# Filler matmuls at the start, weight work moved within the first batches, and next x's maximum and x2's low part moved within the batch loop

## What is computed

```python
x = layernorm(x + L0(x, adj))    # y = (adj @ x + x) @ W0 + b0; y / |y|
x = layernorm(x + L1(x, adj))    # S = 8 tanh((xq)(xk)^T / sqrt(128) / 8); P = exp(S) * adj
                                 # (P / rowsum P) @ x @ v
x = layernorm(x + L2(x, adj))    # (s_i + s_j + adj * w_r + g_b) @ x @ W2 + b2
x = layernorm(x + L3(x, adj))    # relu(x@W3[0] + L@x@W3[1] + (2 L@L - 1)@x@W3[2] + b3)
```

## Time and profile before

| | |
|---|---|
| median of 3 runs | 712.55 us (712.53, 712.55, 714.25) |
| the profiled execution | 713.7 us |
| its span, first to last instruction | 711.4 us |
| TensorE busy | 636.5 us, 89% |
| VectorE busy | 589.1 us, 83% |
| ScalarE busy | 414.6 us, 58% |
| GpSimd busy | 74.0 us |
| mean granted TensorE clock | 0.97 of full |

### The profile page before, as it was taken

How to read it: one execution, slowest core, us unless ns; L and a number is a source line. 1 busy time by engine, 2 the same in 40 slices (tenths; PEclk the granted TensorE clock), 3 DMA queues, 4 the chain that set the end, 5 groups by cost and what they waited for, 6 DMA issues and landing times. The chain is left out here.

```text
span 711.4 us, 17445 instructions
## 1 busy us (share of the span) xinstructions
PE 636.5 (89%) x7398; PEld 477.7 (67%) x7398; DVE 589.1 (83%) x1521; ACT 414.6 (58%) x711; POOL 74.0 (10%) x49
## 2 busy tenths in 40 slices
PE   4598577899899998999899998999899999879894
PEld 2355444559666895669666895769666995548794
DVE  5868998778898898998898888998898888879535
ACT  6369559425584657836593658646693649423512
POOL 0111110002000210012001100012001100021002
PEclk9899888999999999999999999999999999989998
DMA  9520000001000020002000020002000010000102
GB/s 333 188 89 1 1 1 1 1 1 33 1 1 2 2 61 1 2 1 61 2 2 2 2 61 1 1 2 61 1 2 2 2 32 1 2 0 3 31 3 60
DMA packets 12446, 18.75 MB, mean 26 GB/s; under 512 B 592, under 2 KB 9040, under 8 KB 12368
## 3 DMA queue, kind: packets, MB, share of 16 engines
q1 hardware_dynamic: 12368, 17.63, 7.5%
HBM read 13.44 MB, written 4.19 MB: 25 GB/s over the span
## 5 line engine op out<-in xcount | busy, mean ns | idle before, releaser
L238 POOL TENSOR_TENSOR small<-small,minus_half 128x8 f32<-128x8 f32 x39 | 69.6, 1788 | 616.0 <-DVE small L564 317.8
L836 DVE TENSOR_TENSOR att<-att,adjT 128x1024 f32<-128x1024 f32 x64 | 78.1, 1221 | 16.2 <-ACT att L385 15.7
L383 ACT ACTIVATE att<-r,coef 128x1024 f32<-128x1024 f32 x64 | 70.4, 1101 | 18.7 <-PE r L1213 18.1
L841 DVE SCALAR_TENSOR_TENSOR p_lo<-p_hi,att 128x1024 f16<-128x1024 f16 x64 | 77.9, 1220 | 0.0
L279 ACT ACTIVATE p_hi<-att 128x1024 f16<-128x1024 f32 x64 | 66.9, 1045 | 18.2 <-DVE att L836 18.2
L1211 PE MATMUL r<-xq,a_hi 128*128 128x128 f16 x448 | 76.0, 219 | 0.0
L1212 PE MATMUL r<-xq,a_hi 128*128 128x128 f16 x448 | 76.0, 219 | 0.0
L1213 PE MATMUL r<-xq,a_lo 128*128 128x128 f16 x448 | 76.0, 219 | 0.0
L1211 PE MATMUL r<-rs,a_hi 128*128 128x128 f16 x448 | 75.8, 219 | 0.0
L1212 PE MATMUL r<-rs,a_hi 128*128 128x128 f16 x448 | 75.8, 219 | 0.0
L1213 PE MATMUL r<-rs,a_lo 128*128 128x128 f16 x448 | 75.8, 219 | 0.0
(11 more groups left out here) (380 smaller groups left out, 2092.7 us busy)
## 6 DMA issues: line engine op xcount, KB each, us to landing
adjT<-in_adj_t SPq DMA_DIRECT2D x8, 512.0 KB, 8.3
x<-in_x SPq DMA_DIRECT2D x7, 512.0 KB, 4.7
out<-outb SPq DMA_DIRECT2D x7, 512.0 KB, 3.4
pq<-in_adj SPq DMA_DIRECT2D x2, 512.0 KB, 8.3
u<-in_adj SPq DMA_DIRECT2D x2, 512.0 KB, 9.3
tmp<-in_adj SPq DMA_DIRECT2D x2, 512.0 KB, 10.0
x2s<-in_adj SPq DMA_DIRECT2D x2, 512.0 KB, 10.5
outb<-in_x SPq DMA_DIRECT2D x1, 512.0 KB, 11.3
```

What stands on the lines that cost most here:

```text
L238: return nc.gpsimd.tensor_tensor(dst, src, minus_half[:], ALU.pow)
L383: nc.scalar.activation(att[:, s], dst[:], ACT.Tanh, scale=c_tanh).then_inc(S["th"], 1)
L836: tt(att[:, s], att[:, s], adjT[:, t, :], ALU.mult).then_inc(S["pm"], 1)
L841: stt(p_lo[:, s], p_hi[:, s], -LO_UP, att[:, s], ALU.mult, ALU.add).then_inc(S["pl"], 1)
```

## The change

It moves instructions within the lists of the engines, and adds a few:

- TensorE: filler matmuls (`keep_busy`) of 512 columns, whose result nothing reads: 9 before the first x maximum's sum, 2 after it, 11 before the first product of x, 15 after layer 0's first projection. The first weights' sum stands ahead of chunk 3 in place of chunk 4, the second (w2, w3) ahead of the second scores of batch 0, layer 0's projection of batch 1 ahead of them too, and the sum for x of batch 2 in batch 1's attention.
- The factor in front of the exponential is no longer its bias: ScalarE multiplies adjT by it in place (`scale_adj`, eight copies, each after that chunk's a_lo is made).
- ScalarE: `v_scaled(0)` and the last row sum stand behind the first exponential; the row sums are taken in groups of 3, 3, 1, 1; `bias_rows` moves from batch 1's attention to the start of `back(1)`.
- VectorE, start: y of batch 1 and the scales of w2 and w3 stand ahead of and just behind the first mask, the weights of layer 3 in the wait for the first root and their maxima behind the splits of m and v, the first norm's shift ahead of batch 1's y0 low part; the maximum of x of batch 2, and the splits of w2 and w3, move from between the batches into batch 1's attention.
- VectorE, every `back`: the maximum of x of batch i + 2 ahead of the second `end_sum` (it stood at the start of the next front), and `x2_lo` ahead of `ln_shift(0, i + 1)` (it stood at the end).

```diff
         coef = sb("coef", [P, 8])
-        c_w0, c_tanh, c_v, c_l2, c_u, c_o, c_exp = (coef[:, j:j + 1] for j in range(7))
+        c_w0, c_tanh, c_v, c_l2, c_u, c_o = (coef[:, j:j + 1] for j in range(6))
         deg, dis, dis2, root_deg, eps_deg, r_scale, q_scale = (sb(n_, [P, C]) for n_ in ("deg", "dis", "dis2", "root_deg", "eps_deg", "r_scale", "q_scale"))
...
         names = ("w_in bc_in wq_in iu_ok x_in x1_in ident_ok const_ok m_cp w3_c m_mm w_max w_sum w_red w_ok wj_c "
-                 "adj_hi adj_lo deg_ok sc_ok b3_ok "
+                 "adj_hi adj_lo adj_up deg_ok sc_ok b3_ok "
                  "norm_sq norm_r dis_ok x_max x_sum x_st x_hi x_lo "
...
+            def scale_adj(first, last_):
+                for c in range(first, last_):
+                    act.wait_ge(S["adj_lo"], c + 1 if c < C - 1 else C + 1)
+                    copy(adjT[:, c], adjT[:, c], LO_UP * P_UP).then_inc(S["adj_up"], 1)
             def degrees(first, last_):
...
                 act.wait_ge(S["th"], t8 + t + 1)
-                nc.scalar.activation(att[:, s], att[:, s], ACT.Exp, scale=TANH_CAP, bias=c_exp).then_inc(S["ex"], 1)
+                nc.scalar.activation(att[:, s], att[:, s], ACT.Exp, scale=TANH_CAP).then_inc(S["ex"], 1)
...
+                scale_adj(0, 3)
                 y0_hi(0, 0, r1[:, half(0)])
                 y0_hi(0, 1, r1[:, half(1)])
+                degrees(0, 3)
                 x0_hi(1)
-                degrees(0, 4)
+                scale_adj(3, C)
+                degrees(3, 6)
                 act.wait_ge(S["p0_mm"], 2)
                 y0_hi(1, 0, m7[:])
-                degrees(4, 6)
                 norm(0, 0, xas[0], V_CHUNKS)
...
                 g_hi(0, r2)
-                degrees(7, 8)
                 y0_hi(1, 1, av[:, 2])
                 v_hi(0, r1)
-                v_scaled(0)
-                act.wait_ge(S["const_ok"], 1)
                 for t in range(C):
                     exponent(0, t)
+                    if t == 0:
+                        v_scaled(0)
+                        degrees(7, 8)
                     if t >= 1:
...
                         copy_x2(0)
-                    if t == 4:
-                        bias_rows()
                 p_hi_part(1, C - 1)
...
                 last = i >= 2
+                if not last:
+                    bias_rows()
                 act.wait_ge(S["y0_mm"], 2 * (i + 1))
...
             nc.vector.memset(one_sj[:, :, 0:1], 1.0)
-            nc.vector.memset(c_exp, float(np.log(LO_UP * P_UP)))
+            nc.vector.memset(x1T[:, 0, half(0)], 1.0)
             nc.vector.memset(vhis[0][:, :, D:D + 1], 1.0)
...
-            def second_max():
+            def third_layer_weights():
                 ch = Count(dve, S["w3_c"], 0, 2)
...
                 ch.end()
+            def later_max():
                 weights_max(3, (w2_sb[:], w3c.rearrange("p k d -> p (k d)")))
...
                 x0_lo(1)
+                third_layer_weights()
                 rows.residual()
...
                 weights_split(1, 2)
-                y0_lo(1, 0, m7[:])
+                later_max()
                 ln_shift(0, 0)
                 ln_norm(0, 0, xas[0])
+                y0_lo(1, 0, m7[:])
                 x1t_lo(0, r1)
...
                 rows.begin()
+                rows.y_half(0, r2)
+                rows.y_half(1, r2)
+                dve.wait_ge(S["adj_up"], C)
                 mask(0, 0)
+                weights_scale(1, slice(3, 5))
+                second_coefs()
                 for t in range(1, C):
...
                     if t == 1:
-                        rows.y_half(0, r2)
-                        rows.y_half(1, r2)
-                    if t == 2:
                         rows.stats_half(0)
...
                         rows.arg()
+                    if t == 2:
+                        row_scales()
                     if t == 3:
-                        row_scales()
-                        second_max()
+                        rows.residual()
                     if t == 4:
-                        rows.residual()
+                        ln_begin(0, 1, xas[1])
                     if t == 5:
-                        ln_begin(0, 1, xas[1])
-                    if t == 6:
                         ln_shift(0, 1)
                         ln_norm(0, 1, xas[1])
-                        weights_scale(1, slice(3, 5))
-                        second_coefs()
+                    if t == 6:
                         gate_weights()
...
                 x1t_lo(1, r0)
-                weights_split(3, 4)
-                w_ch.end()
-                x0_max(2)
                 g_lo(1, r1)
...
                 l_.then_inc(S["e1a"], 1)
-                x0_scale_read(2)
                 mask(1, 0)
...
                 ln_begin(1, 0, xas[0])
+                x0_max(2)
                 mask(1, 1)
...
                 p_lo_part(1, 2)
+                x0_scale_read(2)
                 x0_scales(2)
...
                 p_lo_part(1, 4)
+                weights_split(3, 4)
+                w_ch.end()
                 mask(1, 6)
...
                 l2_ch = Count(dve, S["l2_c"], i - 1, L2_LINKS)
-                if nxt:
-                    x0_max(i + 1)
                 sums_read(i - 1, m7)
...
                 q_part(z_all, i - 1, 1)
+                x2_lo(i)
                 ln_shift(0, i + 1)
...
                 v_lo(i + 1, r1)
+                if i + 2 < B:
+                    x0_max(i + 2)
                 end_sum(i - 1, 1)
                 sj_step(sj_ch, i, 3)
-                x2_lo(i)
...
+            def keep_busy(n):
+                for _ in range(n):
+                    mm(r0[:, half(0)], ident_up[:], x1T[:, 0, half(0)], start=True, stop=True)
+            pe.wait_ge(S["const_ok"], 1)
+            pe.wait_ge(S["iu_ok"], 1)
+            keep_busy(9)
             pe.wait_ge(S["x_max"], 1)
-            pe.wait_ge(S["const_ok"], 1)
             mm(m7[:, 4:5], ones[:], xmax[:], start=True, stop=True).then_inc(S["x_sum"], 1)
+            keep_busy(2)
             pe.wait_ge(S["wq_in"], 16)
...
             pe.wait_ge(S["ident_ok"], 3)
+            keep_busy(11)
...
             pe.wait_ge(S["x_lo"], 1)
-            pe.wait_ge(S["iu_ok"], 1)
             for c in range(C):
-                if c == 4:
+                if c == 3:
                     weights_sum(0, 0, 3)
...
                 layer0_half(0, 1, r1)
+                keep_busy(15)
                 pe.wait_ge(S["x_lo"], 2)
...
                 scores(0, 0)
+                layer0_half(1, 0, r2)
+                layer0_half(1, 1, r2)
+                weights_sum(1, 3, 5)
                 pe.wait_ge(S["v_lo"], 2)
                 scores(0, 1)
-                layer0_half(1, 0, r2)
-                layer0_half(1, 1, r2)
                 next_scores(0, 2)
...
                     next_scores(0, t)
-                    if t == C - 1:
-                        weights_sum(1, 3, 5)
                     attend(0, t - 3)
...
                 attend(0, 7)
-                row_max_sum(2)
                 v_product(1, r0)
...
                 next_scores(1, 4)
+                row_max_sum(2)
                 attend(1, 1)
...
```

## The result

| | before | changed |
|---|---|---|
| median on one chip | 713.28 us (712.53 to 714.25, four runs) | 691.76 us (691.42 to 692.46, four runs) |
| the profiled execution | 713.7 us | 691.9 us |
| its span | 711.4 us | 689.7 us |

The ratio is 0.9694, with a 95% interval of 0.9679 to 0.9710: 21.5 us less, where 17.35 were forecast. On the 712.55 us shown with the kernel before, the ratio gives 690.8 us. The direction was right, and so was the main mechanism, the wait for the maximum. The sum was 4.2 us too small, mainly because the exponential's bias and the last front had no term in it.

The account below looks back on a forecast made before the run. The prediction took the steady loop as TensorE-bound with one hole per batch, two also costing clock, and VectorE's order as pacing the start. Head 5.6 + loop 8.85 + clock 2.9 = 17.35 us off 713.7: 696.4 us, range 691.5 to 702.5.

Parts of the forecast that it names:

- The steady loop: Five full batches: TensorE's 2.13 us wait for the maximum closes, but tile 5 limits the gain to 1.77 us each, 8.85 us.
- The clock: Two of five batches also lost clock behind the wait for the maximum; these losses vanish too, 2.9 us, bounds 0 and 3.5.
- x2's low part in the root's wait: Every back: x2's low part runs on VectorE during GpSimd's root; priced at 0, bounds 0 and 0.9 us per batch.
- own last step: To 144 us: about 7.8 us at attention's residual, less 1.13 and 1.76 returning in batch 1; a 0.4 us root wait vanishes.
- (a): Load phase: the weights' sum before chunk 3 removes VectorE's 2.43 us wait at 18.02, gaining 2.45 us.
- Step (b): Start: the first norm's shift no longer waits 1.55 us behind the next batch's high part; gain 1.45 us at the first transpose.
- Step (c): Batch 0's attention: low-scaled v and one row sum go behind ScalarE's first exponential; second tile gains 2.1 to 2.2 us.
- Step (d): Batch 0's dense VectorE stretch: y halves, third-layer weights with maxima, and scales, 4.13 us, move into earlier idle time.
- Better than summed: Rival, chance 0.11: TensorE gains the full 2.13 us and the head 8 us; 691.5 us and below.
- The stall at the end sum: Rival, chance 0.08: maximum finds x late or second score waits in full; 1.14 of 1.77 us return; 702 or 705.
- the slow root: Rival, chance 0.10: GpSimd's root and x2's low part exclude each other, 0.9 us in each of six batches; 701.8 us.
- one rival: Chance 0.15: TensorE idles after the second filler and clock drops, or adj comes late; head gains 0 to 2, 700 to 702.

Follow-up runs that it names:

- e3: Kernel before with the maximum ahead of the second end sum and x2's low part in the root's wait, bias and old start kept: 702.04 us, 0.9834.
- e9: Kernel before with both loop moves and the exponential without its bias (adj scaled at the start), old start otherwise, no fillers: 698.81 us, 0.9796.
- e2: Kernel before with only the exponential's bias exchanged for in-place scaling of adj by ScalarE: 712.32 us, 0.9983.
- e4: Changed kernel with the exponential's bias back and no scalings of adj: 695.24 us, 0.9742.
- e1: Kernel before with only the maximum of the next x moved ahead of the second end sum: 705.03 us, 0.9883.
- e5: Changed kernel with x2's low part back at the end of the loop: 696.96 us, 0.9768.
- e6: Changed kernel with x2's low part ahead of the second q sum, so that it starts before the root: 696.94 us, 0.9765.
- e7: Changed kernel without any filler matmuls (37 left out): 694.49 us, 0.9734.
- e11: Changed kernel with the first weights' sum back ahead of chunk 4, fillers kept: 693.10 us, 0.9729.
- e8: Changed kernel with 24 fillers in place of 15 behind layer 0's projection: 691.88 us, 0.9702.
- e10: Changed kernel with third-layer weights, their maxima and scales, and batch 1's y halves back among batch 0's tiles: 697.04 us, 0.9774.

## Where the prediction was right, and the step that failed

**The steady loop.** Right: the hole of 2.13 us was what the batch lost, and the maximum stands free where it was put. The end sum moved by the 0.3 us forecast, and no second score waits for it. Right too, by e3: with the exponential as it was, TensorE waits at tile 5 and the batch lasts 77.1 us.

**The step that failed** is "exchanging the exponential's bias for them changes nothing in its 1.15 us". The exponential took 1.06 us; in starts, an exponential and the tanh behind it lie 0.97 us apart instead of 1.06. The chain from ScalarE through VectorE to the low part of tile 5, which set the 1.77 us, is shortened at each exponential on it, and the wait of 0.20 us vanishes (e3 and e9). Of the 0.38 us between these two loops the other 0.18 lies in what the profile counts as TensorE's busy time (76.84 and 76.65 us); no row shows where. The whole 2.17 us come, not 1.77: 5 x 0.4 = 2.0 us of the missing 4.2. e2 and e4 show the price from both sides: 0.2 us a batch while the maximum is waited for, 0.4 once it isn't. The prediction had a row for the exponential with its bias and none without, and should have given the term bounds.
The Trainium skill (ScalarE: Activation LUTs, section What ACT_TABLE_LOAD costs) says that each operand given as one number per partition adds some 93 ns to an ACTIVATE. The trace agrees: 0.09 us from 1.15 to 1.06.

**The clock.** Right: 2.98 us for 2.9 forecast. Both losses went with the holes, and in e1 and e5, whose holes are half as long, none came back. That the trace of before holds two of them is in part luck: e2's, with the same five holes, has one.

**x2's low part in the root's wait.** Right, at nothing; e5 gives the move 5.2 us with the rest in place, and e6 shows how near its cost was: started 0.6 us earlier, with the q sum behind it, it is worth nothing.
The Trainium skill (SBUF — State Buffer, section SBUF: two separate sides) would have whichever starts first hold the shared port pair for the whole instruction. e6 comes near it for one order: the root starts 0.17 us behind the low part, which ends at 246.67, and lasts 1.5 us from there. The changed kernel speaks against it for the other: the low part starts inside the root and takes its usual 1.22 us.

**The head.** 6.55 us against 5.6, of which 0.85 is that x happened to land earlier (the first maximum at 4.43 in this trace, 5.28 in that of before). What is left, 5.7 us, is the forecast's number, but not by all of its steps, and in part by luck. (The prediction's own last step gives 7.8 - 1.13 - 1.76 + 0.4 = 5.3, or 5.7 with TensorE's slack.)

"The filler matmuls let chunk 0 start at the full clock, which I count at nothing, since VectorE's low parts set the pace there" was wrong: without them TensorE's chunks come late, and the sum that VectorE wants stands in TensorE's list behind them (e7, 1.96 us of wait; 2.7 us in the end). The 2.45 us of (a) are real, but need both the position and the fillers (e7, e11).

Step (b) brought 0.7 us of its 1.45 in this trace: the transposes start 4.15 us behind the root instead of 4.87, since TensorE did the first part of x's product for batch 1 at half clock; in e8 and e11, at full clock throughout, it is 3.3. Step (c) made up for it: the second mask comes 2.3 us earlier without x's landing, where 2.15 was forecast. Step (d) was right in size by its 4.1 us (e10).

By medians the start is worth 7.05 us (e9 to the changed kernel). By the traces of the same two kernels it is 5.94 to the first root and 0.95 in the end section, which in e9's profile is longer with the same work, at a mean clock of 0.94 instead of 0.95. What moved the clock there wasn't tried.

**The last front** had no term, and gained 1.08 us (54.86 to 53.78 from the last root to the last projection). No maximum is taken in that stretch, so in the kernel before TensorE's wait of 0.91 us for x2's low part stood there in the open. e1 leaves it at 54.86; with the move too (e3) it is 54.24, and without the bias (e9) 53.77. So 0.6 us are the move's and 0.5 are again the bias's.

Together: 2.0 (bias in the five batches), 1.1 (last front), 0.85 (x's landing) and 0.24 (end) are 4.2 of the 4.35 us by which the spans' 21.7 exceed 17.35; the clock and the rest of the head add 0.1 each.

**The rivals.** "Better than summed" held, but by the bias and the last front, not by a head of 8 us. The prediction is not at one with itself here: it gave this case, 691.5 and below, 0.11, and what lies below 691.5 0.08. The stall at the end sum, the slow root and the late high part of x2 did not come. The head did find the low clock behind its last fillers (0.50 from 30 to 33 us), as one rival said, but it took 0.85 us (e8) and not the 3.6 to 5.6 that this rival let it take.

## What to carry to other kernels

When a wait is removed, the next limit decides how much of it comes, so an edit that is worth nothing beside the old wait (the bias, 0.2 us a batch) has to be priced on the loop without it (0.4); list every operand that the diff takes from an instruction on that chain. For each position that an instruction gives up, look in every stretch whether something else waited for it there: the last front's wait of 0.91 us stood in the trace. And where an engine's clock is low, ask for the instruction of it that another engine waits for, not only whether it sets the pace on the whole; measure what it costs between two fixed instructions of the traces, since a median can hide 0.8 us (e8).

## What the runs showed of the hardware that was not expected

- With a bias given per partition each of the 64 128x1024 exponentials takes 1.15 us, without it 1.06.
- GpSimd's pow of 128x8 takes 1.64 us, and 2.55 when a VectorE instruction with both inputs in SBUF started 0.17 us ahead of it (e6). One that starts 0.44 us behind it costs neither of the two anything (the changed kernel).
- Idle times of TensorE of 2.1 us were followed by a lower granted clock (0.72 over 6 us) in two of five cases in the kernel before and in one of five in e2, those of 2.0 us near 28 us in three of six traces. Behind those of 0.9 to 1.1 us in e1 and e5, twelve in all, it stayed at 1.00.
- 512-column matmuls whose result nothing reads, placed in TensorE's idle time at the start, took 2.7 us off the whole kernel (e7). Nine more of them kept the clock at 1.00 near 30 us and shortened the way from the first norm's root to the last by 0.8 us in the trace, which the medians don't show (e8).
- In the kernel without them TensorE's first products, from 9.80 to 14.88 us, ran at half its rate (starts 0.43 us apart, not 0.22), though the granted clock of the profile reads 1.00 there. In this stretch the rate has to be read from the distance of the matmuls.
